# Decay rows made in two batch halves inside project and attention, first rows loaded at project's end, k stored through GpSimd's queue, expert products ahead of gathers

## The reference, cut to what matters

```
Q, K, V = proj(wq, bq), proj(wk, bk), proj(wv, bv)      # each x @ w.T + b
Q, K = rope(Q), rope(K)
scores = einsum('bhqd,bhkd->bhqk', Q, K) / sqrt(HD)
pd = sigmoid(x.mean(axis=1) @ wd.T + bd)                # one number per batch and head
log_decay = log(1.0 - exp2(-5.0 - 8.0 * pd))
scores = scores + pos_diff[None, None] * log_decay[:, :, None, None]
attn = softmax(scores);  out = attn @ V                 # heads side by side
on = (out - mu) / sqrt(var + 1e-05) * gamma + beta      # per batch and head
return silu(x @ wg.T + bg) * on @ wo.T + bo
```

```
h = gelu(einsum('becd,edh->bech', tokens, w1) + b1);  y = einsum('bech,ehd->becd', h, w2) + b2
out = zeros_like(x).at[b_idx, sel_idx].add(y * gate_vals[..., None])
```

## Time and profile before

| | us |
|---|---|
| median of 3 runs | 3446.3 |
| lowest and highest | 3445.3, 3448.44 |
| the profiled execution's own time | 3451.66 |
| span of the profiled execution | 3449.9 |
| busy PE, DVE, ACT, POOL | 3035.3, 2443.9, 1752.3, 1381.5 |

### The profile page before, as it was taken

How to read it: one execution, slowest core, us unless ns; L and a number is a source line. 1 busy time by engine, 2 the same in 40 slices (tenths; PEclk the granted TensorE clock), 3 DMA queues, 4 the chain that set the end, 5 groups by cost and what they waited for, 6 DMA issues and landing times. The chain is left out here.

```text
span 3449.9 us, 51677 instructions
## 1 busy us (share of the span) xinstructions
PE 3035.3 (88%) x17140; PEld 2018.0 (58%) x17140; DVE 2443.9 (71%) x5884; ACT 1752.3 (51%) x3844; POOL 1381.5 (40%) x1366
## 2 busy tenths in 40 slices
PE   6999966999872999998759998889799999999989
PEld 3555555888640444444648886689545555555557
DVE  5888865777564777775757775223499999999964
ACT  2545313333441899997323333235366666666644
...
GB/s 115 1 1 1 1 49 77 38 54 1 29 115 76 27 30 27 30 27 20 88 77 38 48 1 27 1 1 1 1 1 1 1 1 1 1 1 1 1 13 38
DMA packets 106567, 91.43 MB, mean 27 GB/s; under 512 B 15373, under 2 KB 96147, under 8 KB 104000
## 3 DMA queue, kind: packets, MB, share of 16 engines
...
...
## 5 line engine op out<-in xcount | busy, mean ns | idle before, releaser
L2427 ACT ACTIVATE m_x_hT<-m_x_hid,wm_b 128x260 f32<-128x260 f32 x512 | 244.3, 477 | 422.6 <-PE m_x_hid L2366 422.6
L1318 POOL TENSOR_TENSOR c_tE<-c_tE,c_tDm 128x256 f32<-128x256 f32 x512 | 372.2, 728 | 139.6 <-ACT c_tE L1278 125.8
L1201 DVE TENSOR_REDUCE c_tM<-c_tpa 128x2 f32<-128x512 f32 x512 | 330.3, 682 | 130.9 <-PE c_tpa L1103 129.9
L1278 ACT ACTIVATE c_tE<-c_tpb 128x512 f32<-128x512 f32 x512 | 309.7, 606 | 43.4 <-PE c_tpb L1120 43.4
L2366 PE MATMUL m_x_hid<-m_x_xg,wm_w 128*128 128x260 f32 x1024 | 319.7, 396 | 1.2 <-DVE m_x_cols L2310 1.2
L2374 PE MATMUL m_x_yp<-m_x_hT,wm_w 128*128 128x260 f32 x1024 | 311.5, 388 | 0.0
L1654 POOL TENSOR_TENSOR b_wkv<-b_at,b_rec 128x512 f32<-128x512 f32 x128 | 163.1, 1275 | 306.2 <-DVE b_rec L1590 306.2
L1103 PE MATMUL c_tpa<-c_tK,c_Qm 96*128 96x256 f16 x1024 | 205.5, 284 | 49.4 <-DMA c_Qm<-aug_d 36.3
L1259 ACT ACTIVATE c_tDm<-wc_pos,c_LD 128x128 f32<-128x128 f32 x512 | 209.1, 411 | 20.5 <-PEq L96 20.5
L1120 PE MATMUL c_tpb<-c_Qm,c_tK 101*128 101x256 f16 x1024 | 198.8, 276 | 23.3 <-ACT c_tE L1278 23.3
L2374 PEld LDWEIGHTS m_x_yp<-m_x_hT,wm_w 128*128 128x128 f32 x1024 | 198.0, 193 | 31.5
...
## 6 DMA issues: line engine op xcount, KB each, us to landing
...
c_Qm<-q_d SPq DMA_DIRECT2D x128, 48.0 KB
...
```

The lines of the kernel that those rows point to most:

```text
L1201: nc.vector.tensor_reduce(out=M[:, u % 2, 2 * h:2 * h + 2], in_=pa[:, h % 2], axis=AX.X, op=ALU.max).then_inc(s["max_done"], 1)
L1278: nc.scalar.activation(E[:, h % 8].rearrange("p a q -> p (a q)"), pb[:, h % 2, :], ACT.Exp).then_inc(s["exp_done"], 1)
L1318: nc.gpsimd.tensor_tensor(diag, diag, Dm[:, u % 2, h:h + 1, :].to_broadcast([P, 2, P]), ALU.mult).then_inc(s["dmul_done"], 1)
L2427: nc.scalar.activation(hT[:, e % 2, j, :], hid[:, c % 2, 0:QW], ACT.Gelu, bias=w["m_b1"][:, c:c + 1]).then_inc(s["gelu_done"], 1)
```

## The change

Six edits. (1) The decay of batches 0 to 15 is computed in project, after group 9's gate product, and that of batches 16 to 31 at the start of attention; the decay block is gone. (2) Project clears K and Qm (on GpSimd) and its SP loads the rows of batches 0, 1, 2 after its last store. (3) The three k stores of a group are issued by GpSimd, one group late; q, k and their low halves have four buffers in place of two. (4) The v bias moves from VectorE in project to the copy in attention's `place`; VectorE's instruction on v becomes a ScalarE copy. (5) The add of `bo` goes to GpSimd in finish, and each residual waits for its group. (6) In the experts, the products of e come ahead of gathers, turns and scatters of e; GATHERS is one step earlier; on VectorE `y_out` comes before `take` and `moments` before the last `y_out`.

```diff
+    def parts(self, dve, half):
+        nc, s = self.nc, self.s
+        full, part = self.full, self.part
+        dve.wait_ge(s["back"], 32 * (half + 1))
+        at_least(dve, s["r_out"], 64 * half)
+        rep = self.L4[:, self.blocks(half)][:, :, None].to_broadcast([P, self.HL, P])
...
+        for r in range(2):
+            dve.wait_ge(s["parts"], 4 * half + r + 1)
+            nc.vector.tensor_tensor(part[:, 2 * r + 1], full[:, r], part[:, 2 * r], ALU.subtract).then_inc(s["parts"], 1)
...
+    def load(self, sp, b):
...
+        nc.sync.dma_start(self.K[0:QROWS, u], scr["k"].rearrange("r m g t -> (r m) g t")[:, :, at]).then_inc(self.came[u], 16)
...
+            nc.sync.dma_start(self.Qm[rows, u, hh:HB:HG, :], scr["q"][hh][:, :, at]).then_inc(self.came[u], 16)
+        nc.sync.dma_start(self.Qm[QROWS + 1:KROWS, u, :, 0:P], scr["aug"][:, bass.ds(b, 1)].rearrange("r b h q -> r (b h) q"))\
...
-        retention_decay(nc, k, tag + "d", w, scr, XM, LD, Qm)
-        retention_attend(nc, k, tag + "t", w, scr, VO, LD, Qm, mv)
+        with ExitStack() as inner:
+            decay = Decay(nc, inner, tag + "d", w, scr, XM, LD)
+            rows = Rows(nc, inner, tag + "r", w, scr)
+            retention_project(nc, k, tag + "p", w, scr, VO, XM, decay, rows)
+            retention_attend(nc, k, tag + "t", w, scr, VO, LD, decay, rows, mv)
...
             def work(g, slot, i):
-                dve.wait_ge(s["v_done"], g + 1)
-                nc.vector.tensor_tensor(VO[:, bass.ds(g * GT, GT), :], vp[:].rearrange("p (a d) -> p a d", a=GT),
-                                        w["c_bv"][:, None, :].to_broadcast([P, GT, D]), ALU.add).then_inc(s["v_out"], 1)
                 dve.wait_ge(s["th_done"], g + 1)
+                at_least(dve, g_out[g % 2], 16 * (g // 2))
+                nc.vector.scalar_tensor_tensor(out=gate[:, g % 2, :], in0=th[:], scalar=1.0, in1=gateb[:], op0=ALU.add,
+                                               op1=ALU.mult).then_inc(s["gate_done"], 1)
                 at_least(dve, out_sem[slot], OUTS * i)
-                nc.vector.scalar_tensor_tensor(out=gate[:, slot, :], in0=th[:], scalar=1.0, in1=gateb[:], op0=ALU.add,
-                                               op1=ALU.mult).then_inc(s["gate_done"], 1)
+                at_least(dve, k_out[slot], K_OUTS * i)
                 for j in range(2):
                     dve.wait_ge(s["hi_done"], 2 * g + j + 1)
                     nc.vector.tensor_tensor(lo[:, slot, j, :], rot[:, j, :], hi[:, slot, j, :], ALU.subtract).then_inc(s["lo_done"], 1)
...
             for g in range(NG):
                 turn_pairs(g, g % 2)
-                work(g, g % 2, g // 2)
+                work(g, g % NS, g // NS)
+                if g == DECAY_AT + 3:
+                    decay.parts(dve, 0)
 
         @block.gpsimd
         def _(pool):
+            def store(g, slot):
+                at = bass.ds(g * GW, GW)
+                pool.wait_ge(s["lo_done"], 2 * g + 2)
+                for term, ks in enumerate((hi, hi, lo)):
+                    rows = slice(term * HD, (term + 1) * HD)
+                    nc.gpsimd.dma_start(scr["k"][:, rows, :, at].rearrange("r d g t -> r (d g) t"), ks[:, slot, 1, :]).then_inc(k_out[slot], 16)
...
+            def clear(n):
+                u, half = n // 2, n % 2
+                pool.wait_ge(rows.s["zeroed"], n + 1)
+                nc.gpsimd.memset(rows.Qm[:, u, half * HB // 2:(half + 1) * HB // 2, :], 0.0).then_inc(rows.s["zeroed"], 1)
+
+            nc.gpsimd.memset(rows.K[96:KROWS], 0.0).then_inc(rows.s["zeroed"], 1)
+            for n in range(3):
+                clear(n)
             for g in range(NG):
+                if 3 <= g < CLEARS:
+                    clear(g)
                 for j in range(2):
                     pool.wait_ge(s["cs_done"], 4 * g + 2 * j + 2)
                     at_least(pool, s["lo_done"], 2 * g - 1 + j)
                     nc.gpsimd.tensor_tensor(rot[:, j, :], cs[:, 2 * j, :], cs[:, 2 * j + 1, :], ALU.add).then_inc(s["rot_done"], 1)
+                if g > 0:
+                    store(g - 1, (g - 1) % NS)
+            store(NG - 1, (NG - 1) % NS)
+            for q in k_out:
+                pool.wait_ge(q, K_OUTS * NG // NS)
...
+            def values(g):
+                act.wait_ge(s["v_done"], g + 1)
+                nc.scalar.copy(VO[:, g * GT:(g + 1) * GT, :], vp[:].rearrange("p (a d) -> p a d", a=GT)).then_inc(s["v_out"], 1)
+
             def split(g, slot, i):
                 at_least(act, out_sem[slot], OUTS * i)
+                at_least(act, k_out[slot], K_OUTS * i)
                 for j in range(2):
                     act.wait_ge(s["rot_done"], 2 * g + j + 1)
                     nc.scalar.copy(hi[:, slot, j, :], rot[:, j, :]).then_inc(s["hi_done"], 1)
@@ -909,7 +1046,10 @@
                 if g + 2 < NG:
                     normalise(g + 2, g % 2)
                 gates(g)
-                split(g, g % 2, g // 2)
+                if g == DECAY_AT:
+                    decay.logs(act, 0, vp[0:HB, 0:decay.HBT])
+                values(g)
+                split(g, g % NS, g // NS)
...
+                if g == DECAY_AT:
+                    pe.wait_ge(s["sum_done"], DECAY_AT - 1)
+                    decay.mean_product(pe, 0, vp[0:HB, 0:decay.HBT])
+                    pe.wait_ge(decay.s["th"], 1)
...
-                nc.sync.dma_start(scr["gate"][:, at], gate[:, slot, :]).then_inc(out_sem[slot], 16)
-
-                for term, (qs, ks) in enumerate(((hi, hi), (lo, hi), (hi, lo))):
+                nc.sync.dma_start(scr["gate"][:, at], gate[:, g % 2, :]).then_inc(g_out[g % 2], 16)
+
+                for term, qs in enumerate((hi, lo, hi)):
                     rows = slice(term * HD, (term + 1) * HD)
                     nc.sync.dma_start(scr["q"][:, rows, :, at].rearrange("r d g t -> r (d g) t"), qs[:, slot, 0, :]).then_inc(out_sem[slot], 16)
-                    nc.sync.dma_start(scr["k"][:, rows, :, at].rearrange("r d g t -> r (d g) t"), ks[:, slot, 1, :]).then_inc(out_sem[slot], 16)
-            for i in range(0, NG // 2):
-                for u in range(2):
-                    store(i * 2 + u, u)
+            sp.wait_ge(rows.s["zeroed"], 1)
+            for u in range(NB):
+                nc.sync.dma_start(rows.K[QROWS:KROWS, u].rearrange("r g t -> r (g t)"), w["c_kaug"]).then_inc(rows.s["const"], 16)
+            for g in range(NG):
+                store(g, g % NS)
+                if g == DECAY_AT:
+                    decay.logs_out(sp, 0)
+                if g == DECAY_AT + 1:
+                    decay.logs_back(sp, 0)
+                if g == DECAY_AT + 3:
+                    decay.rows_out(sp, 0)
+            sp.wait_ge(rows.s["const"], 16 * NB)
+            sp.wait_ge(rows.s["zeroed"], 1 + CLEARS)
+            decay.rows_landed(sp, 0)
+            sp.wait_ge(out_sem[0], OUTS)
+            sp.wait_ge(k_out[0], K_OUTS)
+            sp.wait_ge(out_sem[1], OUTS)
+            sp.wait_ge(k_out[1], K_OUTS)
+            for b in range(NB - 1):
+                rows.load(sp, b)
             for q in out_sem:
-                sp.wait_ge(q, OUTS * NG // 2)
...
+            decay.logs_out(sp, 1)
+            decay.logs_back(sp, 1)
             for b in range(B):
                 put_max(b // NB, b % NB)
+                if b == 3:
+                    decay.rows_out(sp, 1)
                 if b + NB - 1 < B:
                     load_rows((b + NB - 1) // NB, (b + NB - 1) % NB)
...
+            decay.mean_product(pe, 1, misc[0:HB, 3, 0:decay.HBT])
...
+                if b == 0:
+                    pe.wait_ge(decay.s["th"], 2)
...
+                    if t == 10 and b == 2:
+                        decay.parts(dve, 1)
...
+                if h == 0 and b == B // 2:
+                    act.wait_ge(decay.s["back"], 64)
...
+                nc.scalar.activation(VO[:, bass.ds(b * 2, 2), :], misc[:, 1:3, :], ACT.Identity, bias=w["c_bv"][:, 0:1]).then_inc(s["vo_done"], 1)
...
+                dve.wait_ge(s["biased"], g + 1)
...
+            for g in range(NG):
+                xg = k.X[:, g * GT:(g + 1) * GT, :]
+                nc.gpsimd.tensor_tensor(xg, xg, w["c_bo"][:, None, :].to_broadcast([P, GT, D]), ALU.add).then_inc(s["biased"], 1)
...
-        GATHERS = {0: (0,), 1: (1,), 2: (2,), 3: (3,), 4: (4,), 5: (5, 6), 6: (7,), 7: ()}
+        GATHERS = {0: (0,), 1: (1,), 2: (2,), 3: (3, 4), 4: (5, 6), 5: (7,), 6: (), 7: ()}
+        ONEHOTS = {0: 0, 1: 1, 2: 2, 4: 3}
...
 
             def quad(q):
                 u = q % 2
-                if q + 1 < NQ:
-                    onehot(q + 1, 1 - u, 0)
                 for e in range(NE):
-                    if q + 1 < NQ and e % 2 == 0 and e // 2 + 1 < QB:
-                        onehot(q + 1, 1 - u, e // 2 + 1)
+                    if e in ONEHOTS and q + 1 < NQ:
+                        onehot(q + 1, 1 - u, ONEHOTS[e])
+                    if e in BEHIND and q < NQ:
+                        select(q, BEHIND[e])
```

(26 more changed lines are left out.)

204 lines of the change are left out of this document (107 added, 97 removed).

## The result

| | us | ratio to before, 95% interval |
|---|---|---|
| before | 3446.2 | |
| after, median of four runs | 3392.3 | |
| after, median of three, see below | 3387.3 | 0.9832 (0.9802 to 0.9862) |
| after, the profiled execution (span 3379.4) | 3381.2 | |

The account below looks back on a forecast made before the run. SP's store queue was taken to pace project, then a hole before attention and TensorE gaps in the experts; -26 - 34.6 - 32 + 7 + 2 = -83.6 gives 3368.1 profiled, 3363 against the median; range 3334 to 3400.

Parts of the forecast that it names:

- rival A: Project's pace stays 9.07: written memory is slow, or all k stores fall on the same engines; 3389 us, chance 0.13.
- B: Rival in project: GpSimd becomes the bound at 1.75 us per issue, group 7.8 us; +26, 3389 us, chance 0.12.
- Project: Moving k off SP's queue takes a group from 9.07 to 6.3 us; gain 26 after extras, bounds +3 and -35.
- engine chain of 6.3 us: Project's next limit after SP's queue: the engines' own work, 6.3 us per group (6.0 to 6.6).
- The extras: Work added to project: clears 5 us, other clears beside the first turn 0.7, logs 4.5, VectorE's `parts` 2.
- D: Rival: slower than before, GpSimd issues at 4 us each make a project group 15.2 us; 3484 us, chance 0.03.
- The hole: Last low half to first `scores_k`: 68.95 us before, 34.4 after; gain 34.6, bounds -28 to -37.
- four stores of 0.5: Term of the hole: SP's remaining stores after project's last low half, 2.1 us before the row loads.
- The path through the logs and back: In the hole: SP's logs to HBM and back end about 13 us in, maxima want SP at 15; next to be late.
- Experts: Both stages: products fill TensorE's 2.15 us gaps at quad changes and the clock stays up; gain 32, bounds -20 and -34.
- Attention: Second-half `parts` cost VectorE about 2 us once, felt by score products; bias in `place` free; loss 2.
- Finish: GpSimd's `bo` adds slow VectorE's `z = za * gate`, 2.02 us per group for 10 groups; loss 7, bounds 0 and 12.

Follow-up runs that it names:

- wide_before: The kernel before with q and k laid out term outermost in memory, so a store is one list of 128 rows: 3398.3 us, ratio 0.9863.
- k_wide: The changed kernel with the term-outermost memory layout for k alone, q's stores keeping the old shape on SP's queue: 3377.0 us, ratio 0.9813.
- wide_after: The changed kernel with q and k laid out term outermost, q still on SP's queue and k on GpSimd's: 3369.1 us, ratio 0.9760.
- spread_bo: The changed kernel with second-half decay instructions one per batch, and the `bo` adds on VectorE at project's end: 3382.2 us, ratio 0.9809.

## Why the prediction was right, and where it was wrong

**Sum.** 3363 forecast, 3387 measured (3392 as the median of all four), inside the range; 3368.1 against 3381.2 in terms of the profile. The time is nearer to the 3389 of rivals A and B than to the forecast, without either of them being what happened: it is the sum of two gains that fell short, a loss that was larger and an experts part that gave more.

**Project, the step that failed:** "Moving k leaves 640 of 1024 KB on SP's queue: 9.07 x 0.625 = 5.7 us per group". The bytes on SP's queue do not set the pace: with k gone from it the group took 9.3 us once the queue was full, and with k still on it, but all stores spread, 6.33 (wide_before). In before, SP's stores waited for four engines that carried all of q and k. The 13.5 us that were gained came from six groups at 6.3 to 6.7; the nine behind them took 2 us more than nine at 9.07. Why GpSimd's stores in the old shape cost so much once they had left SP's queue is open (k_wide). I had this as rival A at 0.13. Its first half, the memory, is refuted by wide_before, and its second ("or all k stores fall on the same engines") does not fit the packets of after. The engine chain of 6.3 us, was right to 0.03 us. The cost: 20.9 us over wide_after in this stretch.

**The extras were sized too high, and hid a part.** Clears 5, logs 4.5, decay rows 2, lead-in 0.7: 12.2 forecast. In wide_after they are 3.6 in all; clears between the adds cost nothing at 6.3.

**The rule on engines.** 192 rows on each of four engines at the 47.2 ns of a 1 KB packet in before are 9.06 us per group, near the measured 9.07; the gate's rows come beside them. The Trainium skill's rule ("DMA: Bandwidth & Descriptors", "Why a DMA increments its semaphore by 16 and not by 1": the outermost sizes of both sides decide how many engines a transfer gets) agrees with these runs for SP, by the four packets at once. For GpSimd the same section has transfers of fewer than 16 engines take them in turn. The up to twelve packets at once in after agree with that; but by that alone k_wide would have changed nothing but the loads, and it took the groups from 9.3 to 7.0. And the Trainium skill's other section on that page, "Issuing engines are not separate DMA queues", which I weighed as a rival, was nearer to this case than I allowed: two queues gave 128 GB/s where one gave 112, and nothing more once the stores were spread.

**GpSimd as the bound (B, D).** 0.70 us per store against my 1.0; neither rival came near.

**The hole.** 45.6 in place of 34.4 us. The row loads (1033.13 to the meeting at 1048.2, 15.1 against 14.2) and the lead-in (17.3 against 17.5) are as worked out. The term of 2.1 us for "four stores of 0.5" was the wrong one: SP's backlog made it 13.1. In wide_after, without a backlog, it is 2.2. The path through the logs and back was not late.

**Experts.** The mechanism was right: the gap, the moments and the clock behind it. 32 forecast, 37.7 in the rows by undoing it. The ten full quads behind the first of each stage gave 34.7 us, close to my 32.8, but partly by luck: seven of them in before were of the long kind (44.7 us), where I had read five, and the last two quads of each stage, which I did not look at, took 3.5 us more in after than before. My bank wait of 1 us in e = 4 did not show. The rest is the clock in the stage's first microseconds, which falls out differently from run to run.

**Attention.** +8.2 against +2. The step "`parts` of the second half cost VectorE about 2 us once": they cost 3.4 us of VectorE, a wait of TensorE of 3.29, and then its clock, 5.5 together; spread_bo takes all of that back. And "the bias in `place` is free" was wrong: 2.7 us.

**Finish.** +8.6 against +7. `c_fz` takes 1.16 and not 1.36 beside the adds, steps of 1.69 in place of 2.02, but VectorE's small coefficients before them grew as well (1.24 us for one of 0.24 before).

**Untouched rest.** -8.5 us in stages with the same code: 2.7 ahead of the first gather, at a mean clock of 0.90 in both, and 5.9 behind the last moments, at 0.93 in place of 0.92. I count it to the run and not to the change, which no experiment settles.
